# Three passes of a mixer beside edge units: columns split 3, 5, 9 instead of 0, 6, 11, with changed order, bias and stores

## What is computed

```python
edge_index = jnp.stack([src, dst])
xn = _layernorm(x, axis=-1)
x = x + _L0_gnn_ref(xn, edge_index, ...) + _L0_mix_ref(xn[None], ...)[0]
x = x + _L0_ffn_ref(_layernorm(x, axis=-1)[None], ...)[0]
```

```python
q = jax.nn.softmax(split(x @ Wq) * scale, axis=-1)
k = jax.nn.softmax(split(x @ Wk) * scale, axis=-2)
v = split(x @ Wv)
context = jnp.einsum('bhnd,bhne->bhde', k, v)
out = jnp.einsum('bhnd,bhde->bhne', q, context)
return out @ Wo + bo                                   # x = x + this
x = x + (gelu(h @ W1[i] + b1[i]) @ W2[i] + b2[i])      # h: layer norm of x
```

## Time and profile before

| | |
|---|---|
| median of 3 runs | 15123.15 us (15119.13 to 15126.68) |
| the profiled execution | 15134.86 us, its span 15133.0 us |
| TensorE (matmuls), VectorE, ScalarE, GpSimd busy | 85%, 45%, 46%, 20% of the span |
| granted clock, mean | 0.957 |

### The profile page before, as it was taken

One profiled execution on the slowest core, in us unless ns is written; L12 is line 12 of the kernel. 1 busy time (PEld: TensorE's weight loads), 2 busy tenths in 40 slices (PEclk: granted clock), 3 DMA queues, 4 the chain that ended last, 5 costly groups with the idle time before them and its releaser, 6 DMA issues. The chain is left out here.

```text
span 15133.0 us, 1967100 instructions
## 1 busy us (share of the span) xinstructions
PE 12931.8 (85%) x904808; PEld 11428.5 (76%) x904808; DVE 6867.8 (45%) x47499; ACT 6946.3 (46%) x42309; POOL 2960.0 (20%) x4500
## 2 busy tenths in 40 slices
PE   3687776877669999999999999999999999999998
PEld 2566565766558888888888888888888888888886
DVE  4755747556553333333333333333333333333335
ACT  2454544645414444444444444444444444444443
POOL 4483764737700000000000000000000000000000
PEclk7898888988889999999999999999999999999998
DMA  3342543424420000000000000000000000000000
GB/s 80 97 143 71 148 123 98 145 72 144 136 94 3 2 2 2 2 2 2 2 2 2 2 2 2 2 2 2 2 2 2 2 2 2 2 2 2 2 2 19
DMA packets 673156, 542.56 MB, mean 36 GB/s; under 512 B 537744, under 2 KB 588954, under 8 KB 660765
## 3 DMA queue, kind: packets, MB, share of 16 engines
q1 hardware_dynamic: 450480, 316.45, 7.3%
q0 software_dynamic: 221600, 223.50, 6.1%
q10 hardware_dynamic: 934, 0.99, 0.0%
HBM read 286.52 MB, written 252.14 MB: 36 GB/s over the span
## 5 line engine op out<-in xcount | busy, mean ns | idle before, releaser
L1477 PE MATMUL p_g<-ring,wh 128*32 128x16 f32 x800000 | 8204.4, 186 | 700.3 <-DVE ring L1576 613.6
L1477 PEld LDWEIGHTS p_g<-ring,wh 128*32 128x32 f32 x800000 | 7592.2, 109 | 1475.3 <-DVE ring L1576 1156.3
L1518 ACT ACTIVATE cell<-p_g 128x3 f32<-128x3 f32 x12500 | 2181.8, 175 | 5555.5 <-PE p_g L1477 5555.5
L1570 DVE CUSTOM_DVE_ANT_1 cj<-cell 128x4 f32<-128x4 f32 x12500 | 2035.0, 163 | 5664.2 <-ACT cell L1518 5664.2
L1611 POOL COPY hist<-ring 128x6 f32 x2501 | 475.7, 190 | 10377.5 <-POOLq L1610 10377.5
L1521 ACT ACTIVATE tc<-cell 128x1 f32<-128x1 f32 x12500 | 2482.6, 199 | 0.0
L422 POOL DMA_INDIRECT eb<-node_tab,eidx x1650 | 2242.1, 1359 | 622.8 <-issue 448.3
L1576 DVE SCALAR_TENSOR_TENSOR ring<-og,tc 128x1 f32<-128x1 f32 x12500 | 1998.7, 160 | 774.8 <-ACT tc L1521 2.1
L1523 ACT ACTIVATE og<-p_g 128x1 f32<-128x1 f32 x12500 | 2043.2, 169 | 2.2 <-PE p_g L1477 2.0
L1451 PE MATMUL p_g<-xq,idn 128*32 128x24 f32 (+3 forms) x80032 | 1614.7, 189 | 61.4 <-PEq L1464 15.8
L1451 PEld LDWEIGHTS p_g<-xq,idn 128*32 128x32 f32 x80032 | 1254.4, 110 | 231.7 <-issue 15.9
(11 more groups left out here) (221 smaller groups left out, 6870.7 us busy)
## 6 DMA issues: line engine op xcount, KB each, us to landing
edge_tab<-eb SPq DMA_DIRECT2D x96, 1391.1 KB
edge_tab<-eb SPq DMA_DIRECT2D x96, 758.8 KB
eb<-node_tab,eidx POOLq DMA_INDIRECT x1650
xp_tab<-xo SPq DMA_DIRECT2D x50, 500.0 KB, 2.6
xq<-xp_tab SPq DMA_DIRECT2D x1251, 8.0 KB, 1.7
xq<-xp_tab SPq DMA_DIRECT2D x1250, 12.0 KB, 1.7
x<-w_in SPq DMA_DIRECT2D x8, 1024.0 KB
out<-ot SPq DMA_DIRECT2D x25, 250.0 KB
```

The source lines that it names most:

```text
L1477: m = pe.matmul(to[32 * q:32 * q + 32], wh[:, k, D * q + 32 * c:D * q + 32 * c + 32], ring[:, (s - 1) % TS, k:k + 1].broadcast_to([128, w] ...
L1518: act.activation(cell[:, s, k, 0:6:2], gate_at(h, u, k)[:, :, 0], ACT.Tanh).then_inc(l_s[k], 1)
L1570: dve.tensor_tensor_reduce(cj[:, k, :].rearrange("p (a b) -> p a b", a=2), cell[:, s, k, 0:4].rearrange("p (a b) -> p a b", a=2), cell[:, ...
```

## The change

The units become 3, 5 and 9 columns in passes A, B and C (`UNITS`), so that pass A has edge work too: `edges(0, ...)` on VectorE between `k_max` and `context`, `edge_weigh` at the end of ScalarE's step, stores on SP and gathers on GpSimd. In units of 3 the pieces of the next maximum begin one column earlier (`at`). On ScalarE the exponentials of pass A stand ahead of the values' copy; TensorE's wait for that copy (`m_vs`) moves from ahead of the context to ahead of the next values. The attention's bias is no longer added to every double tile but, divided by the 8 heads, to the output matrix `cxo`. A store becomes two, of 112 and of 13 rows.

```diff
-UB, UC = 6, 11
+UNITS = (3, 5, 9)
+UC, UL = max(UNITS), sum(UNITS)
...
-                    pool.wait_ge(e_free[s], 16)
-                    pool.sem_inc(e_free[s], -16)
+                    pool.wait_ge(e_free[s], 32)
+                    pool.sem_inc(e_free[s], -32)
...
+                    at = 1 if n > 3 else 0
...
-                        if coming and j == 1:
+                        if coming and j == at:
...
-                    sp.dma_start(edge_pj[:, ds(c0, n), :], eb[s][:, 0:n, :]).then_inc(e_free[s], 16)
+                    for rows in by_rows:
+                        sp.dma_start(edge_pj[rows, ds(c0, n), :], eb[s][rows, 0:n, :]).then_inc(e_free[s], 16)
...
                         coming = begin(forward_loads(layer))
+                        units(sp, layer, 0, lambda place: edge_store(sp, place))
                         barrier("sp", sp)
-                        units(sp, layer, 0, lambda place: edge_store(sp, place))
+                        units(sp, layer, 1, lambda place: edge_store(sp, place))
...
                         def context(vb):
                             pe.wait_ge(m_ekr, 1)
                             pe.sem_inc(m_ekr, -1)
-                            pe.wait_ge(m_vs, 1)
-                            pe.sem_inc(m_vs, -1)
...
                         if not last:
                             norm_pe(pe)
+                        if not first:
+                            pe.wait_ge(m_vs, 1)
+                            pe.sem_inc(m_vs, -1)
...
-                        act.wait_ge(m_v, 1)
-                        act.sem_inc(m_v, -1)
-                        act.activation(flat(vs[:, b]), p_v[0:R, :], ACT.Copy).then_inc(m_vs, 1)
                         act.wait_ge(m_mx, 1)
...
                         a.then_inc(m_ek, 1)
+                        act.wait_ge(m_v, 1)
+                        act.sem_inc(m_v, -1)
+                        act.activation(flat(vs[:, b]), p_v[0:R, :], ACT.Copy).then_inc(m_vs, 1)
+                        if unit:
+                            edge_weigh(act, unit_place(0, 0, unit))
...
                             k_max()
+                        edges(0, s, unit)
+                        if not first:
                             context(1 - b)
-                        bias_dve(dve, own, s, bob)
...
-                        dve.tensor_copy(flat(cxo[:]), p_e[:, 0:KC * D]).then_inc(s_dve, 1)
+                        for k in range(KC):
+                            a = dve.scalar_tensor_tensor(cxo[:, k, :], bob[:], 1.0 / HEADS, p_e[:, k * D:(k + 1) * D], ALU.mult, ALU.add)
+                        a.then_inc(s_dve, 1)
```

More of the change, by code:

```diff
@@ L49 @@
 DEPTH, HEADS, DH, FF = 4, 8, 32, 1024
-U0 = (EC - DEPTH * NSTEP * (UB + UC)) // 2
-assert 0 < U0 <= UC and 2 * U0 + DEPTH * NSTEP * (UB + UC) == EC and NSTEP % NSLOT == 0
+U0 = (EC - DEPTH * NSTEP * UL) // 2
+assert 0 < U0 <= UC and 2 * U0 + DEPTH * NSTEP * UL == EC and NSTEP % NSLOT == 0
 FC = FF // 128
@@ L80, in unit_place @@
     slot, rnd, nth = unit
-    n = (UB, UC)[which]
-    first = layer * (NSTEP * (UB + UC)) + nth * n + (2 * U0 + which * NSTEP * UB)
+    n, ahead = UNITS[which], sum(UNITS[:which])
+    first = layer * (NSTEP * UL) + nth * n + (2 * U0 + NSTEP * ahead)
     per = NSTEP // NSLOT
-    upto = layer * (per * (UB + UC)) + (rnd + 1) * n + (which * per * UB + (U0 if slot >= 2 else 0))
+    upto = layer * (per * UL) + (rnd + 1) * n + (per * ahead + (U0 if slot >= 2 else 0))
     return slot, first, n, upto
@@ L493, in edge_sum @@
                             dve.tensor_copy(eb[s][:, 0:n, D], eden[:, s, f:])
-                        if coming and j == 1:
+                        if coming and j == at:
                             found = max_found(dve, own, coming)
-                        if coming and j == 2:
+                        if coming and j == at + 1:
                             parted = max_parted(dve, own, coming, found)
-                        if coming and j == 3:
+                        if coming and j == at + 2:
                             max_ready(dve, coming, parted)
@@ L532, in gps_kernel @@
                 b1s = sb(ctx, "b1s", [128, FC])
-                bob, b2b = sb(ctx, "bob", [R, 2, D]), sb(ctx, "b2b", [R, 2, D])
+                bob, b2b = sb(ctx, "bob", [128, D]), sb(ctx, "b2b", [R, 2, D])
                 blk = sb(ctx, "blk", [128, 128])
@@ L653, in attention_loads @@
                         pairs = [(wab[:, i], w[layer:layer + 1].rearrange("a (k p) n -> p (a k) n", p=128)) for i, w in enumerate((wq, wk, wv, wo))]
-                        pairs += [(bob[:, j, :], bcast(one(bo, layer), R)) for j in range(2)]
+                        pairs += [(bob[:], bcast(one(bo, layer), 128))]
                         pairs += [(ln[:, i, :], one(v, layer).rearrange("(k p) -> p k", p=128)) for i, v in ((0, g1), (1, b1n))]
@@ L688, in _ @@
                         coming = begin(attention_loads(layer + 1)) if layer + 1 < DEPTH else 0
-                        units(sp, layer, 1, lambda place: edge_store(sp, place))
+                        units(sp, layer, 2, lambda place: edge_store(sp, place))
                         if coming:
@@ L698, in _ @@
                     for s in range(NSLOT):
-                        pool.nop().then_inc(e_free[s], 16)
+                        pool.nop().then_inc(e_free[s], 32)
                     for place in AHEAD:
@@ L704, in _ @@
                         units(pool, layer, 1, lambda place: edge_gather(pool, place))
+                        units(pool, layer, 2, lambda place: edge_gather(pool, place))
                     for s in range(NSLOT):
-                        pool.wait_ge(e_free[s], 16)
-                        pool.sem_inc(e_free[s], -16)
+                        pool.wait_ge(e_free[s], 32)
+                        pool.sem_inc(e_free[s], -32)
                 @block.tensor
@@ L877, in pass_b @@
                         if unit:
-                            edge_weigh(act, unit_place(0, 0, unit))
+                            edge_weigh(act, unit_place(0, 1, unit))
                         if last:
@@ L894, in pass_c @@
                         if unit:
-                            edge_weigh(act, unit_place(0, 1, unit))
+                            edge_weigh(act, unit_place(0, 2, unit))
                     with act.Fori(0, DEPTH):
@@ L1028, in pass_b @@
                         q_max()
-                        edges(0, s, unit)
+                        edges(1, s, unit)
                         if not first:
@@ L1041, in pass_c @@
                             norm_dve(dve, s + 1)
-                        edges(1, s, unit)
+                        edges(2, s, unit)
                         if not first:
```

## The result

The changed kernel took **14610.4 us** (median of 4 runs, 14605.3 to 14612.3) against 15122.7 for the kernel before (15119.1 to 15126.7). The ratio is 0.9661, 95% interval 0.9647 to 0.9674: 512 us faster, where 440 were forecast.

What follows compares the result with a forecast made beforehand. GpSimd's gather issue was taken to bound pass C, VectorE pass B, while GpSimd rested in pass A. Gains 393 + 58 - 14 + 3 = 440 us from 15,123.2 gave 14,685 us; own range 14,630 to 14,790, wider range 14,615 to 14,850.

Steps and rivals of the forecast that it cites:

- Pass C: Units of 9 columns at 15.95 us each on GpSimd; pass takes 375 us, saving 393 us over four layers.
- TensorE's floor of 14.1 us: In pass C, up-projections follow each other every 14.11 us at TensorE's own pace, making a pass of 361 us.
- the disturbance that shrinks with the run: Pass C: gathers held up by VectorE's accumulation run; going from 14 to 10 cuts it from 2.5 to 1.45 us a unit.
- the late arrival of the last units: Pass C: the twenty-fourth unit is 20.6 us late; VectorE absorbs 6.8, leaving the pass 13.8 us above its floor.
- Pass B: VectorE bounds it; one column fewer saves 0.6 us a step, 58 us over 24 steps and four layers.
- Part 4: Stores split into 112 and 13 rows: a store takes 4 us, gathers land within some 3 us, 3 us gained at the end.
- the second rival: Split stores spread nothing, gathers land 9.2 us late, a pass C unit takes 17.0 us: 14,830 us total, chance 0.15.
- part 2: Pass A, exponentials ahead of the values' copy: no gain or loss booked, step stays 6.5 us, between 6.0 and 10.2.
- part 3: Bias moved to the output matrix: 25 additions of 0.69 us leave VectorE in pass A; about 0.5 us a layer added.
- The booked 14 us of loss: Output-matrix bias work plus edge work in pass A's first and last step: 3.5 us a layer lost, 14 us in all.
- Rival 1: Pass C gathers undisturbed, 14.11 us a step throughout: 55 us less than forecast, 14,630 us total, chance 0.18.
- Rival 3: Pass A's buffer loop of store, gather and landing paces it, step 12 us: 15,210 us, slower than before, chance 0.05.

Runs made afterwards that it cites:

- b_order_bias: The kernel before with only the exponentials ahead of the values' copy and the bias in the output matrix, no edge work in pass A: 15060.1 us, ratio 0.9952.

## Why the prediction was right or wrong

**Pass C, right.** The bound (GpSimd's issue at 1.52 us a column), TensorE's floor of 14.1 us, the disturbance that shrinks with the run, the late arrival of the last units and the slack of VectorE were much as worked out: a unit of 15.6 us where 15.95 was written, and 372.9 to 375.2 us a pass where 375 was written. The 17 us above the forecast in this line are 5.5 us from taking the third and fourth pass before as the second, 4 us from passes slightly shorter than 375, and 7 us at the barriers into the next layer, which I had taken as unchanged.

**Pass B, right in kind.** VectorE's work fell by one column and the pass by 10 to 13 us a layer, 46.5 in all. The term was 58, 0.6 us a step; it measured 0.48, less than the 0.54 of the two accumulations alone.

**Part 4, right.** Landing within 3 us, and worth 121 us in the changed kernel; the second rival, in which it does nothing, is out. The store itself was taken as 4 us and lasts 5.4 to 6.3. That it helps pass A as well was not seen.

**Pass A, wrong, and it is the step that failed.** The text said of part 2 "I book no gain and no loss: the step stays 6.5 us" and of part 3 that the additions "leave a VectorE that had idle time behind them". The first was a choice at the cautious end of a range that began at 6.0. The second was a misreading of the earlier trace rows. The idle 2.44 us lie ahead of the context, the bias addition behind it, and from the context on VectorE's work up to the normalised tiles is on the way to TensorE's next values. An engine that waits 2.4 us a step can still be in a loop that sets the step, with the work behind its wait. Laid out as a loop, the trace of before gives it, from the context's end at 406.45 us on: 0.16 us to VectorE's first operation, 1.63 over the context and the bias addition to the start of the copy (the last 0.29 of it a wait, which is 0.26 also where the turned keys are long ready), 1.49 for the copy and the normalised tiles up to their transposes, 3.23 for transposes, values and the next context, in all 6.51, the same as the step. Taking 0.69 us off gives 5.8; b_order_bias measured 5.9. The booked 14 us of loss became a gain of 62.8; with 62.8 in its place the sum is 517, against the 512 measured.

That the edge units would nearly fit into VectorE's wait was right: they cost 4.3 us a layer.

**The rivals.** Rival 1, no disturbance left, gave 14,630, near the measured time for the wrong reason: the disturbance is there (2.66 us), and pass C is 13 us above its floor. The rule of the Trainium skill ("SBUF — State Buffer", Who interferes with whom) behind it, a lock held for one instruction at a time, does not by itself give these rows: a gather that is caught waits out the rest of a run of six, eight, ten or fourteen accumulations and ends 1.1 us behind the run. Rival 3 was seen at work only with one-piece stores, and small.

## What to carry to other kernels

Idle time on an engine is room only for work that is put into the wait; work behind the wait, in the same step, may be on the loop that sets the pace. So follow each loop around once, through every engine, and write down its length: where two are equal, as here, a change of one shows little, and a change of both more than the sum. And where GpSimd issues gathers beside VectorE, cut VectorE's long uninterrupted runs of accumulations in pieces.

## What the runs showed that was not expected

A gather issued by GpSimd can wait out the rest of a run of accumulations on VectorE, and not one of them only. Those that were held took 3.3 us on average beside runs of 14, 2.5 beside 10, 2.0 beside 8 and 1.8 beside 6, with 1.22 undisturbed; some that began early in a run passed it. Moving three small operations into the middle of a run was worth 54 us (0.4%), at no cost elsewhere. It goes the other way too: beside gathers, a copy on VectorE took 0.47 us instead of 0.29. And a store of 125 rows in one piece slowed not only itself but also the gathers: they landed 9.2 us after issue in the median, and 3.0 us with the same bytes in 112 and 13 rows.
